# Loading the expert numbers of four tiles with one TensorE instruction, without the check of their range

## The reference

```
x = x + attn_a(layernorm(x))   # windowed attention, 16 heads, and an MLP 128 -> 512 -> 128
x = x + ffn(layernorm(x))
x = x + attn_b(layernorm(x))   # windows of 128, one head
x = x + ffn(layernorm(x))

def ffn(x):                    # 8 experts, W1 (8, 512, 128), W2 (8, 128, 512), Wr (8, 128)
    probs = softmax(einsum('btd,ed->bte', x, Wr))
    vals, idx = top_k(probs, 2)
    gate = einsum('btk,btke->bte', vals / vals.sum(-1, keepdims=True), one_hot(idx, 8))
    h = silu(einsum('btd,efd->btef', x, W1))
    y = einsum('btef,edf->bted', h, W2)
    return einsum('bte,bted->btd', gate, y)
```

## Time and profile before

| | |
|---|---|
| median of 3 runs | 565.09 us (564.62 to 568.42) |
| the profiled execution | 566.33 us, of which the span from the first to the last instruction is 564.5 us |
| TensorE, matmul | 488.1 us busy, 86% of the span |
| TensorE, weight load | 378.0 us, 67% |
| VectorE, ScalarE, GpSimd | 292.4, 250.6, 247.5 us |
| mean granted clock of TensorE | 0.934 |

### The profile page before, as it was taken

One profiled execution on the slowest core, in us unless ns is written; L12 is line 12 of the kernel. 1 busy time (PEld: TensorE's weight loads), 2 busy tenths in 40 slices (PEclk: granted clock), 3 DMA queues, 4 the chain that ended last, 5 costly groups with the idle time before them and its releaser, 6 DMA issues.

```text
span 564.5 us, 12563 instructions
## 1 busy us (share of the span) xinstructions
PE 488.1 (86%) x4071; PEld 378.0 (67%) x4071; DVE 292.4 (52%) x960; ACT 250.6 (44%) x529; POOL 247.5 (44%) x229
## 2 busy tenths in 40 slices
PE   1989999999999999899979999937998499999970
PEld 0647776868666887766867787715777297787750
DVE  5556495948796789746731010057577743010115
ACT  7754566573645444333322323346663122232333
POOL 7134262435332464641676253621146567343460
PEclk9998898999898999989889999969998679999995
DMA  7865292967396337011132310040001223311007
GB/s 234 255 145 82 61 171 63 171 135 104 86 148 134 66 95 130 15 34 39 39 87 82 82 35 24 36 149 2 1 19 40 66 68 82 86 53 35 21 30 224
DMA packets 66594, 48.36 MB, mean 86 GB/s; under 512 B 7861, under 2 KB 60615, under 8 KB 66534
## 3 DMA queue, kind: packets, MB, share of 16 engines
q1 hardware_dynamic: 61430, 36.99, 30.8%
q0 software_dynamic: 5104, 10.57, 5.3%
HBM read 16.14 MB, written 27.59 MB: 77 GB/s over the span
## 4 chain that ended last, share of the span: by engine, by line
PE 70%; DVE 11%; issue 6%; DMA 5%; POOL 3%; SPq 2%; ACT 2%; POOLq 0%; DVEq 0%; ACTq 0%
PE PS L817 14%; PE PS L658 9%; PE PS L801 7%; PE PS L803 4%; PE PS L645 3%; PE PS L710 3%; PE PS L620 3%; PE PS L802 3%; PE PS L639 3%; PE PS L556 2%; DMA X<-in_x 2%; PE PS L602 2%; PE PS L668 2%; PE PS L629 2%; SPq L303 2%
## 5 line engine op out<-in xcount | busy, mean ns | idle before, releaser
L507 POOL DMA_INDIRECT YY<-W2R,ID x78 | 77.0, 988 | 81.4 <-ACT W2R L1296 62.8
L451 POOL TENSOR_TENSOR R<-NM,I64B 128x1024 bf16<-128x1024 f32 x32 | 61.4, 1920 | 114.0 <-DVE NM L1464 109.0
L1288 ACT ACTIVATE W2R<-PS 128x512 f32<-128x512 f32 x78 | 46.6, 597 | 125.9 <-PE PS L803 125.8
L817 PE MATMUL PS<-WB,W2R 128*128 x624 | 90.5, 291 | 0.0
L495 POOL DMA_INDIRECT XS<-W1R,SLOT x64 | 64.0, 1000 | 48.0 <-DVE SLOT L1590 31.4
L801 PE MATMUL PS<-QKM,WA 128*128 128x128 bf16 x312 | 71.7, 232 | 9.6 <-issue 4.4
L817 PEld LDWEIGHTS PS<-WB,W2R 128*128 128x128 f32 x624 | 77.8, 197 | 2.4 <-issue 0.2
L1741 DVE COPY QKM<-PS 128x1024 bf16<-128x1024 bf16 (+1 forms) x20 | 13.5, 677 | 123.6 <-PE PS L780 123.6
L803 PE MATMUL PS<-QKM,WA 128*128 128x128 bf16 x312 | 71.7, 232 | 0.0
L802 PE MATMUL PS<-QKM,WA 128*128 128x128 bf16 x312 | 69.5, 225 | 0.0
L658 PEld LDWEIGHTS PS<-VB,PF 128*128 128x128 f32 x512 | 60.1, 193 | 9.2 <-issue 9.2
(11 more groups left out here) (207 smaller groups left out, 871.2 us busy)
## 6 DMA issues: line engine op xcount, KB each, us to landing
XS<-CST SPq DMA_DIRECT2D x30, 520.0 KB, 9.9
QKM<-XS SPq DMA_DIRECT2D x78, 65.0 KB
QKM<-QK SPq DMA_DIRECT2D x64, 72.0 KB, 2.1
QKM<-YY SPq DMA_DIRECT2D x16, 256.0 KB, 4.8
W2R<-in_W POOLq DMA_DIRECT2D x1, 2048.0 KB, 12.3
YY<-W2R,ID POOLq DMA_INDIRECT x78, 2.2
XS<-CST SPq DMA_DIRECT2D x2, 585.0 KB, 9.0
XS<-W1R,SLOT POOLq DMA_INDIRECT x64
```

The lines of the kernel that those rows point to most:

```text
L451: nc.gpsimd.tensor_tensor(R[:, u % 2], NM[:, u % 2].unsqueeze(2).to_broadcast([P, NH, WIN]), I64B[:].unsqueeze(1).to_broadcast([P, NH, WIN ...
L507: pool.indirect_dma_start(out=YY[f], out_offset=to, in_=YS[n % NY][:, i, :], in_offset=None, bounds_check=NPAIRS - 1, oob_is_err=False) \
L817: last = mm(o, HF[n % 3][:, k, :], WB[:, e, k, :].rearrange("p o c -> p (o c)"), start=k == 0, stop=k == KF - 1)
L1288: fn(HF[n % 3], PS[:, n % 3, :].rearrange("p (k s) -> p k s", k=KF), ACT.Silu).then_inc(s["f_hf"], 1)
```

## The change

`choose` takes a group g of up to four tiles in place of a tile t. One instruction loads the group's numbers into as many registers, with the check of their range left out. It is called beside `turned` for the same group: right behind the transposes and ahead of `outputs(t - 2)` where t % 4 is 2; where the group begins a phase, behind `outputs(t - 2)` at t % 4 = 3, where `choose` of the group's first tile stood before. `choose(0)` stays where it was and loads four numbers.

```diff
-                def choose(t):
+                def choose(g):
+                    tiles = GROUPS[g]
                     for i, (_, t0, _) in enumerate(PHASES):
-                        if t == t0:
+                        if tiles[0] == t0:
                             pe.wait_ge(s["f_table"], 2 * (NPH * f + i + 1))
-                    which[t] = pe.value_load(EID[0:1, t:t + 1], min_val=0, max_val=NE - 1)
+                    _, experts_of = nc.values_load_multi_w_load_instructions(
+                        EID[0:1, tiles[0]:tiles[-1] + 1], engines=[mybir.EngineType.PE], min_val=0, max_val=NE - 1,
+                        skip_runtime_bounds_check_because="a count of at most NE experts, clamped to 1 and less 1")
+                    which.update(zip(tiles, experts_of))
...
                     if t < NTILE and t % 4 == 2 + late and t // 4 + 1 < NGRP:
                         turned(t // 4 + 1)
+                        if not late:
+                            choose(t // 4 + 1)
                     if t >= 2:
                         outputs(t - 2)
-                    if t + 1 < NTILE:
-                        choose(t + 1)
+                    if t < NTILE and t % 4 == 3 and late:
+                        choose(t // 4 + 1)
                     routed(t)
```

## The result

| | before | after |
|---|---|---|
| median, us | 564.86 (561.84 to 568.42, 4 runs) | 534.81 (529.97 to 536.87, 4 runs) |
| the profiled execution, us | 566.33 | 529.97 |
| its span, us | 564.5 | 528.2 |
| its mean granted clock | 0.934 | 0.938 |

The ratio of the times is 0.9454, with a 95% interval from 0.9363 to 0.9544. The forecast was 538 us, in a range from 529 to 547. The ten executions of this one kernel spread with the granted clock: 526.0 us at 0.946, 535.4 to 536.9 at 0.919.

What follows compares the result with a forecast made beforehand. TensorE's sequencer, not the array, was taken to pace the tiles. 33.2 us from blocks plus 3.7 from pass ends less 9.6 for group loads gave 27.3 us, so 565.09 became 537.8, rounded to 538, range 529 to 547.

Steps and rivals of the forecast that it cites:

- the load of four: Added group load behind the transposes: 0.96 us each, bounds 0.36 and 1.27, ten exposed, costing 9.6 us.
- The block: Each tile's value load, comparison and assertion hold TensorE's sequencer 0.65 us; 51 exposed blocks removed give 33.2 us.
- paced by the sequencer at 1.75 us: A tile without its block, transposes included, takes the sequencer 1.75 us, still above the array's 1.70.
- 7.4 to 8.3: Sign of being right: groups of four tiles follow each other at 7.4 to 8.3 us in place of 9.60.
- the hidden layer's last matmuls would be spaced by the sequencer: Sign in each tile: first hidden matmuls 0.055 to 0.07 us apart, the last ones at the sequencer's pace.
- The starts of the passes: Tiles 0 to 7 of pass 0 and the first four of pass 1 were counted as gaining 0.
- Gathered rows awaited in the middle of a pass: Sign of being wrong: PE waits there; tile 16's gathers were expected to fit with half a microsecond.
- The tails: GpSimd's last eleven sends ending each pass shrink from 14.71 to 12.85 us: 1.86 us, twice, 3.7 in all.
- Only the hole: Rival: a block is worth only its visible idle in PE; gain 12 to 16 us, about 551 us; chance 0.10.
- Comparisons stay: Rival: only the loads merge, each group keeps 1.2 us beside its load, 12 us less gain, 550 us; chance 0.03.
- Clock: Rival: full clock returns earlier or later in pass 1's start, 1.7 us a pass, 534 to 541; within the main case's 0.82.
- Slower: Rival: the group load ahead of the outputs costs over 3.7 us; at 4.5 us each, 573 us; chance 0.02.

Runs made afterwards that it cites:

- e4_twice: The kernel before with a second full value load behind each one; 607.1 us, ratio 1.0758 to the kernel before.
- e1_single_nocheck: The kernel before with one load per tile where it stood, without comparison and assertion; 543.42 us, ratio 0.9593.
- e8_phase: The changed kernel with one load for each phase of tiles (8, 8 and 23 numbers); 529.26 us, ratio 0.9331 to the kernel before.
- e10_no_wait: The changed kernel without the hidden layer's wait on f_hf from a pass's fourth tile on; 527.97 us, ratio 0.935 to the kernel before.
- e11_combined: The changed kernel without the f_hf wait from the fourth tile, and with phase loads of 8, 8 and 24 numbers; 526.15 us, ratio 0.9253 to the kernel before.
- e12_unaligned: The changed kernel with its table moved by one number, so no load of four is aligned; 533.91 us, ratio 0.9448 to the kernel before.
- e9_widths: The changed kernel with loads of 1 to 23 numbers and small matmuls added behind its last tile, to read load durations; 558.04 us, one execution.
- e5_after_again: The changed kernel, unchanged, measured a second time; 528.26 us, ratio 0.9331 to the kernel before.
- e6_behind: The changed kernel with each group's load behind the outputs of tile t-2 in place of ahead; 528.93 us, ratio 0.9331 to the kernel before.
- e2_group_check: The changed kernel with each number's comparison and assertion kept behind the group's load; 545.07 us, ratio 0.9694 to the kernel before.
- e7_two_waits: The changed kernel with two long-satisfied waits added ahead of each tile's hidden layer; 538.15 us, ratio 0.9503 to the kernel before.
- e3_moved_only: The changed kernel with four full checked value loads in place of each group load; 563.59 us, ratio 1.0002 to the kernel before.

## Why the prediction was right

The mechanism was right. The sequencer, not the array, paced the tiles: twice the blocks cost 0.65 us each (e4_twice), half of a block gone gives half of the gain (e1_single_nocheck), and removing sequencer time stops helping at 6.91 us a group (e8_phase, e10_no_wait, e11_combined), beside the 6.8 that the prediction worked out for the array from the earlier trace rows. One term of its sum was mis-sized, the load of four; the rest by its own steps, in us gained on the profiled executions (starts of hidden layers from the timelines):

| step | by the recorded terms | with the load at 0.39 | measured |
|---|---|---|---|
| pass 0, tiles 0 to 8 | 0 | 0 | 1.4 |
| from tile 8 to 9 | 0 | 0 | -0.8 |
| tiles 9 to 15 | 6 x 0.65 - 0.96 = 2.9 | 3.5 | 3.8 |
| from tile 15 to 16 | 0 | 0 | -0.9 |
| tiles 16 to 33 | 17 x 0.65 - 4 x 0.96 = 7.2 | 9.5 | 9.7 |
| from tile 33 to the last eleven sends | 0 | 0 | 0.3 |
| last eleven sends | 1.9 | 1.9 | 1.8 |
| pass 1, tiles 0 to 4 (clock 0.50) | 0 | 0 | 0.4 |
| tiles 4 to 33 | 28 x 0.65 - 5 x 0.96 = 13.4 | 16.2 | 15.9 |
| from tile 33 to the last eleven sends | 0 | 0 | 0.4 |
| last eleven sends | 1.9 | 1.9 | 1.9 |
| behind the passes | 0 | 0 | -1.1 |
| sum | 27.3 | 33.0 | 32.9 |

**The load of four.** It was taken at 0.96 us, because "four elements are nearer to four loads than to one". That was the step that failed: measured, 334 ns and with the gap of 0.06 us 0.39, near the lower bound of 0.36. Its place in the group is worth 7.29 - 6.92 = 0.37 us (e8_phase), so ten exposed loads cost 3.9 us and not 9.6, and the sum is 33.2 + 3.7 - 3.9 = 33.0. The change's part of the profiled difference is 32.9. That the two meet so closely is in part luck: the steps counted at nothing, from -1.1 to 1.4 us each, cancel to -0.2 (unrounded). The reasoning that most of a load is the reading of an element would have been right for four numbers that aren't aligned: 1002 ns (e12_unaligned). The rows of before hold only loads of one and couldn't show it.

The Trainium skill, "Runtime: NRT & Kernel Launch", section "Instruction fetch mechanics", gives some 200 ns for each register even in bulk. The measured 223 to 238 ns for each further single number, read from SBUF here, lie near it (e9_widths); the aligned four at 338 ns, 8 at 596 and 12 at 857 don't, and there the measurement decides.

**The medians.** 565.09 - 32.9 would be 532.2; the first measurement gave 534.81, the second 528.26, which is 0.7 us below the range of the forecast. The forecast of 538 came that near to the first one in part by the executions at a clock of 0.919, of which it had two of four. That the spread goes with the clock is read from the runs. A part of it may be the wait for tile 16's rows (below), but no trace of an execution of the kernel after at 0.919 was kept, so this isn't shown.

**The block.** 51 exposed at 0.65: confirmed by the table to within 0.3 us in the long stretches, and by e4_twice. That a tile without its block, with its share of the transposes, would still be paced by the sequencer at 1.75 us was half right. With the load out it takes 6.92 / 4 = 1.73, but e11_combined shows this to be the array's floor. The sequencer keeps the last word only with the load in it: 7.29 us a group, just under the 7.4 to 8.3 that the prediction had named. Its sign that the hidden layer's last matmuls would be spaced by the sequencer did not come: all twelve stand 0.055 us apart.

**The starts of the passes.** Counted at nothing, and the gains and losses there cancel to -0.3 in pass 0 (why tile 8 gives back 0.8 us was not followed up). The stretch behind tile 15 lost 0.9 us: "were the group load short, PE would wait some tenths there"; it was short, and PE waits 1.16 us for the gathered rows of tile 16's group. The prediction named the place and took the wait for too small. Gathered rows awaited in the middle of a pass were also one of its own signs of being wrong, and here that sign came true, though it cost the sum only 0.9 us in the profiled execution. PE's transposes came 6.9 us earlier (307.85 to 300.99) where 2.9 were forecast; 3.4 of that is the earlier start of the experts. The wait is not always so short: the same kernel waits 1.80 us in e5_after_again, and the variants from e6_behind on 0.5 (e12_unaligned) to 5.0 (e8_phase). In e6_behind, e8_phase and e10_no_wait, where it is 4.2 to 5.0 us, the clock is at 0.50 for 6.9 us around it, and the mean clock of those executions is 0.918 to 0.923. The kernel before doesn't wait there. So the gathers of tile 16 are what a faster TensorE runs into next in pass 0.

**The tails.** They gave 1.82 and 1.86 us, forecast 1.86; eleven sends back to back, 1.28 to 1.29 apart.

**Rivals.** Only the hole: refuted by the group of 7.29 (it wanted 8.6 or more) and by e10_no_wait, where a wait in front of matmuls that already stood at their full spacing was worth 0.37 us a group. (Its forecast doesn't come out of its own terms: 20.5 - 5 is 15.5 before any tail, so the gain would be 16 to 19 us and not 12 to 16; the measured one is far from both.) Comparisons stay: not on line 790, and e2_group_check shows their price, 8.48 - 7.29 = 1.19 us a group, forecast 1.2. Clock: the first four tiles of pass 1 take 10.20 us at a granted 0.67 where they took 10.62 at 0.57, so the full level came a little earlier, and 0.4 us of the 1.7 that this rival allowed were gained. Slower: the load would have to be 3.7 us.

## What to carry to other kernels

When a TensorE stage uses addresses from registers, list the starts of the sequencer's instructions of one tile: if they leave no hole, each value load, check and wait in that row costs its duration plus a gap of about 0.06 us, although PE shows 95% busy, and a change there can be costed by counting until the array is near its own floor (in e7_two_waits, near that floor, 0.52 of 0.84 us came through). Load numbers in fours that start at a multiple of four, and round odd lengths up. Stop when weight loads are in flight nearly all the time (6.86 of 6.91 us here): behind that, further savings on the sequencer gave nothing. The spacing of the matmuls alone doesn't tell: it was full in the kernel after, and a group still had 0.37 us to give. Then look at what a faster TensorE will run into, here the gathers of tile 16.

## What the runs showed of the hardware that was not expected

A register load of two numbers (537 ns) or three (768) takes longer than one of four (338), when the four start at a multiple of four; four that don't, take 996 to 1002 ns, and 24 aligned ones (1659) less than 23 (2089 to 2647). Within one kernel, executions with mean granted clocks between 0.919 and 0.946 are up to 11 us apart, some 4 us for each 0.01, more than several of the edits tried here were worth. Four checked loads bunched behind the transposes opened holes of 1.65 to 2.31 us in PE's matmuls; behind the two longer ones (2.31 and 2.21 us) the granted clock was 0.50 for 3.4 us, behind the two shorter ones it stayed full (e3_moved_only).
